# A two-layer transformer block on one core: the program's head with the second pair's low parts behind the ninth score step, later weights cast earlier, shift rows moved by head, and one normalisation shared by two engines

## What is computed

```python
x = L0_attn_x                                   # (4, 1024, 128) float32
x = x + _layernorm(attention(_layernorm(x)))
x = x + _layernorm(lora_experts(_layernorm(x)))

def attention(x):                               # 16 heads of 64
    xn = layer_norm(x) * g + b
    q, k, v = xn @ wq + bq, xn @ wk + bk, xn @ wv + bv
    scores = q k^T / 8;  scores = where(tril(ones, k=-1), -inf, scores)
    return softmax(scores) @ v @ w0 + b0 + x
```

## Time and profile before

| what | us |
|---|---|
| three runs | 996.43, 996.57, 998.40 (median 996.57) |
| the profiled execution | 996.35 |
| its span on the core | 994.6 |
| PE, PEld busy | 955.1, 600.4 |
| DVE, ACT, POOL busy | 634.6, 536.1, 701.7 |

### The profile page before, as it was taken

How to read it: one execution, slowest core, us unless ns; L and a number is a source line. 1 busy time by engine, 2 the same in 40 slices (tenths; PEclk the granted TensorE clock), 3 DMA queues, 4 the chain that set the end, 5 groups by cost and what they waited for, 6 DMA issues and landing times.

```text
span 994.6 us, 20388 instructions
## 1 busy us (share of the span) xinstructions
PE 955.1 (96%) x7662; PEld 600.4 (60%) x7662; DVE 634.6 (64%) x1869; ACT 536.1 (54%) x729; POOL 701.7 (71%) x517
## 2 busy tenths in 40 slices
PE   8899999999999999999999999999999999999995
PEld 3555656666666565666665666666666666666563
DVE  6666555555667657566757666756666665756377
ACT  5355546555455565765454565665455546555443
POOL 6378766667767767786676877776588676776752
PEclk9999999999999999999999999999999999999998
DMA  4001110011111000002100201110110200000110
GB/s 114 23 1 24 22 23 14 12 23 44 24 23 44 19 6 23 23 23 45 23 5 20 66 23 23 23 23 2 44 23 24 66 23 23 3 23 24 23 44 21
DMA packets 61837, 26.94 MB, mean 27 GB/s; under 512 B 39084, under 2 KB 53804, under 8 KB 61740
## 3 DMA queue, kind: packets, MB, share of 16 engines
q1 hardware_dynamic: 61708, 25.64, 11.0%
q10 hardware_dynamic: 32, 0.00, 0.0%
HBM read 22.76 MB, written 2.35 MB: 25 GB/s over the span
## 4 chain that ended last, share of the span: by engine, by line
PE 71%; POOL 14%; DVE 7%; ACT 4%; issue 3%; DMA 0%; POOLq 0%; ACTq 0%; DVEq 0%
PE po L770 20%; PE st L755 14%; POOL total L520 12%; PE st L680 9%; PE sc L718 7%; PE st L836 5%; PE st L750 5%; PE sc L780 3%; ACT ring L1048 3%; PE st L695 2%; DVE sc L1246 2%; PE st L696 1%; PE st L697 1%; POOL first_moments L477 1%; DVE least L1249 1%
## 5 line engine op out<-in xcount | busy, mean ns | idle before, releaser
L520 POOL TENSOR_TENSOR total<-total,ring 128x1024 f32<-128x1024 f32 (+1 forms) x313 | 539.0, 1722 | 246.2 <-PE po L770 204.7
L1246 DVE CUSTOM_DVE_ANT_0 sc<-sc,key_mask 128x512 f32<-128x512 f32 (+1 forms) x496 | 230.4, 522 | 142.2 <-PE sc L718 139.4
L1048 ACT ACTIVATE ring<-st 128x1024 f32<-128x1024 f32 (+1 forms) x256 | 228.5, 918 | 167.4 <-PE st L755 149.0
L1249 DVE TENSOR_REDUCE least<-sc 128x1 f32<-128x512 f32 x268 | 170.4, 678 | 74.9 <-PE sc L718 73.1
L770 PE MATMUL po<-ring,v_sb 128*64 128x512 f32 (+3 forms) x1280 | 210.7, 467 | 0.0
L755 PE MATMUL st<-q_high,k_low 64*128 64x512 f32 (+3 forms) x768 | 177.1, 447 | 0.0
L770 PEld LDWEIGHTS po<-ring,v_sb 128*64 128x64 f32 x1280 | 86.9, 137 | 129.5 <-issue 124.4
L718 PE MATMUL sc<-k_high,q_high 64*128 64x512 f32 (+3 forms) x768 | 135.5, 383 | 10.3 <-DVE least L1246 5.2
L755 PE MATMUL st<-q_high,k_high 64*128 64x512 f32 (+3 forms) x768 | 136.9, 343 | 0.0
L755 PE MATMUL st<-q_low,k_high 64*128 64x512 f32 (+3 forms) x768 | 136.8, 341 | 0.0
L718 PEld LDWEIGHTS sc<-k_high,q_high 64*128 64x128 f32 x768 | 69.0, 185 | 81.5 <-issue 64.4
(11 more groups left out here) (184 smaller groups left out, 1256.9 us busy)
## 6 DMA issues: line engine op xcount, KB each, us to landing
inv_row<-sums_dram SPq DMA_DIRECT2D x62, 256.0 KB, 3.9
x_a<-x SPq DMA_DIRECT2D x4, 512.0 KB, 5.1
sums<-sums_row SPq DMA_DIRECT2D x124, 2.0 KB, 2.1
x_b<-x SPq DMA_DIRECT2D x3, 512.0 KB, 5.7
out<-res_b SPq DMA_DIRECT2D x3, 512.0 KB, 4.7
total<-w_pairs SPq DMA_DIRECT2D x1, 1152.0 KB, 6.8
shift_row<-shift_t SPq DMA_DIRECT2D x62, 4.0 KB
x_a<-x SPq DMA_DIRECT2D x2, 256.0 KB, 3.0
```

What stands on the lines that cost most here:

```text
L520: nc.gpsimd.tensor_tensor(so_far, so_far, tile_of(n, s)[:, :, col:col + w], ALU.add).then_inc(s_add, 1)
L1048: nc.scalar.activation(tile_of(n, s)[:, :, 0:w], st[s % 2][:, :, 0:w], ACT.Exp, scale=SCALE).then_inc(s_exp, 1)
L1246: last = nc.vector.tensor_tensor_reduce(bank[:, col:col + w], bank[:, col:col + w], key_mask[:, 0:w], -1.0, 3e38, ALU.add, ALU.min, least[ ...
L1249: last = nc.vector.tensor_reduce(least[:, h, a:a + 1], bank[:, col:col + w], AX.X, ALU.max, negate=True)
```

## The change

It touches five places of the head; the loop over slots is the same.

1. **Order of DVE behind step 8.** `high_w(slice(2, 8), 1)` leaves this place. The low parts of k and q of pair 1 come ahead of `maxima(1, 0)`, k first.
2. **Later weights.** The casts of `high_w(slice(2, 8), 1)` now stand between the two `x_low` instructions, and POOL's `low_w(1, ...)` ahead of `first_shifts`.
3. **Norm shared.** Of the four tiles that DVE normalised, ACT takes two (`s_z_part`). PE's four unread matmuls between the transposes go, and six stand behind them in place of four.
4. **Rows.** `shift` is laid out so that a half's high and low parts of one head stand on eight neighbouring partitions once transposed; one transfer moves both rows (32 instead of 64 counts).
5. **PE.** Pair 1's projections stand in threes between the score steps, without unread matmuls between them. Two unread stand ahead of `("m", 0, 0)`, and four in place of eight ahead of slot 0.

```diff
@@ -208,6 +208,8 @@
         shift = sb("shift", [P, 2, 2, QB], bf16)
+        shift_halves = shift[:].rearrange("p h s i -> p (h s i)").rearrange("p (h a s i) -> p h a s i", h=2, a=2, s=2)
         shift_t = sb("shift_t", [32, P], bf16)
@@ -269,7 +271,7 @@
         s_half, s_later_keys = sem("s_half"), sem("s_later_keys")
-        s_shift_half, s_first_row = sem("s_shift_half"), sem("s_first_row")
+        s_shift_half, s_first_row, s_z_part = sem("s_shift_half"), sem("s_first_row"), sem("s_z_part")
         s_score, s_max, s_shift, s_shift_row = (sem(n) for n in ("s_score", "s_max", "s_shift", "s_shift_row"))
@@ -333,10 +335,9 @@
         def move_first(eng, half, h):
-            for k in range(2):
-                row, i = h * D + k, h * 16 + k * 8 + 4 * half
-                eng.dma_start(shift_row[0][row:row + 1, half * HALF:(half + 1) * HALF], shift_t[i:i + 4, :]
-                              ).then_inc(s_first_row, 16)
+            i = h * 16 + 8 * half
+            eng.dma_start(shift_row[0][h * D:h * D + 2, half * HALF:(half + 1) * HALF], shift_t[i:i + 8, :]
+                          ).then_inc(s_first_row, 16)
@@ -488,15 +489,15 @@
-                blocks = slice(4 * half, 4 * half + 4)
                 if half:
                     pool.wait_ge(s_max, 2 * BLOCK_STEPS)
                     wait_filled(pool, "m", 0, 0)
                 else:
                     pool.wait_ge(s_least, 1)
                 part = least[:, :, QB + 4 * half:QB + 4 * half + 4]
-                pool_link(nc.gpsimd.tensor_copy(shift[:, :, 0, blocks], part))
-                last = nc.gpsimd.tensor_tensor(shift[:, :, 1, blocks], part, shift[:, :, 0, blocks], ALU.subtract)
+                high, low = (shift_halves[:, :, half, a, :] for a in range(2))
+                pool_link(nc.gpsimd.tensor_copy(high, part))
+                last = nc.gpsimd.tensor_tensor(low, part, high, ALU.subtract)
                 last.then_inc(s_shift if half else s_shift_half, 1)
@@ -593,9 +594,9 @@
             gate_constants()
+            low_w(1, slice(2, 8))
             for half in range(2):
                 first_shifts(half)
-            low_w(1, slice(2, 8))
             pool.wait_ge(s_w_low, 2)
@@ -730,7 +731,7 @@
                     need(s_const, 5)
-                    need(s_first_row, 64 * (1 + half))
+                    need(s_first_row, 32 * (1 + half))
                 elif s == 0:
@@ -897,10 +898,10 @@
             turn_four(z_head, 0, st[0][:, 0, :]).then_inc(s_zt, 1)
-            unread(4)
             need(s_z, 1)
+            need(s_z_part, 1)
             turn_four(z_head, 1, st[0][:, 1, :]).then_inc(s_xt, 1)
-            unread(4)
+            unread(6)
@@ -915,25 +916,21 @@
             score(0, 3)
-            project(1, 1, range(0, 2))
+            project(1, 1, range(0, 3))
+            score(0, 4)
+            project(1, 1, range(3, 6)).then_inc(s_fill[0], 1)
+            score(0, 5)
+            project(0, 1, range(0, 3))
+            score(0, 6)
+            project(0, 1, range(3, 6)).then_inc(s_fill[1], 1)
+            score(0, 7)
             unread(2)
-            score(0, 4)
-            project(1, 1, range(2, 4))
-            unread(2)
-            score(0, 5)
-            project(1, 1, range(4, 6)).then_inc(s_fill[0], 1)
-            unread(2)
-            score(0, 6)
-            project(0, 1, range(0, 3))
-            unread(2)
-            score(0, 7)
-            project(0, 1, range(3, 6)).then_inc(s_fill[1], 1)
             fill(("m", 0, 0), "sc")
             score(0, 8)
             unread(6)
             score(1, 0)
             fill(("m", 0, 1), "sc")
-            unread(8)
+            unread(4)
             for t in SLOTS:
@@ -1091,7 +1088,7 @@
                     if part or n == 1:
-                        act.wait_ge(s_first_row, 64 * (1 + n))
+                        act.wait_ge(s_first_row, 32 * (1 + n))
                     reach(act, s_shift_row, 32 * (n - 1))
@@ -1109,6 +1106,9 @@
             norm_apply(1, z_head, x_a, low).then_inc(s_z0, 1)
+            act.wait_ge(s_root, 2)
+            act.wait_ge(s_x[1], 16)
+            norm_apply(1, z_head, x_a, high[:2]).then_inc(s_z_part, 1)
             act.wait_ge(s_cols, 16 * 2)
@@ -1335,11 +1335,13 @@
             dve.wait_ge(s_root, 2)
-            for t in high:
+            for t in high[2:]:
                 root, moved = root_and_moved(1, t)
                 last = nc.vector.tensor_scalar(z_head[:, t, :], x_a[:, t, :], root, moved, ALU.mult, ALU.add)
             last.then_inc(s_z, 1)
             for a in range(2):
+                if a == 1:
+                    high_w(slice(2, 8), 1)
                 half = slice(a * 512, (a + 1) * 512)
@@ -1421,12 +1423,11 @@
                     least_of_two(0)
-            high_w(slice(2, 8), 1)
+            dve.wait_ge(s_high, 4)
+            take(("k", 1, 0), 0)
+            take(("q", 1, 0), 1)
             maxima(1, 0)
-            dve.wait_ge(s_high, 4)
-            take(("q", 1, 0), 1)
-            take(("k", 1, 0), 0)
             for t in SLOTS:
                 c, i = divmod(t, PAIRS)
                 for g in range(3):
```

## The result

The kernel after takes 994.47 us in the median of 17 runs (993.83 to 995.12); the kernel before, beside it, 996.57 (996.37 to 998.40). The ratio is 0.9974, with a 95% interval from 0.9967 to 0.9981: faster by 2.1 us, where 3.0 were forecast. The times of the kernel before lie in two groups, twelve from 996.37 to 997.18 and five from 997.96 to 998.40, so its median depends on how many fall into each. The profiled execution took 994.58 us, its span is 992.8, 1.8 under the one before.

What follows compares the result with a forecast made beforehand. The head's chain up to c0 was taken as the bound, DVE alone from 32.30 to 37.23 us. Terms 0.27 + 0.61 + 1.34 + 0.82 = 3.04 us gave a median of 993.5, range 992.8 to 995.0.

Steps and rivals of the forecast that it cites:

- (a): Rival, head: casts and POOL's masks hold each other up; gain 2.5 to 2.6 us, 994.1; chance 0.18 together with (d).
- (b): Rival, between the two x_low: later weights land late, x_low 1.1 us late; gain 1.7, 994.9; chance 0.13.
- the first term: Between the two x_low: with norm shared and casts in the wait, second x_low at 12.55 for 12.82, 0.27 us gained.
- PE's order: Score steps 5 to 8: PE reaches steps 6 and 7 earlier, so DVE waits less; 0.61 us gained.
- the casts: Behind score step 8: the casts of the later weights leave DVE's chain, where they lay whole; 1.34 us gained.
- the swap: Behind step 8: k and q ahead of S(1,0)'s maxima, cutting DVE's wait for S(1,1) from 1.50 to 0.68; 0.82 us gained.
- The norm: Start of the head: sharing tiles starts the second transpose 0.5 us earlier; ACT's two more tiles cost nothing.
- POOL's order: POOL ahead of the first shift: subtractions end about 27.6, shift asked for at 27.9; costs nothing, 0.3 us to spare.
- The rows in one transfer: Ahead of T(0,0): one transfer there at 32.3, T(0,0) doesn't wait for it; nothing gained or lost.
- T(0,0) neither by the transfer nor by POOL: Sign behind step 8: T(0,0) at 33.0; release by the transfer or by POOL would show the prediction wrong.
- (c): Rival, PE: fewer unread matmuls and new idle stretches drop the clock to 1.2 GHz; slower, up to 1000.3; chance 0.04.
- (d): Rival, behind step 8: S(1,1) sets the pace, the swap's 0.82 falls away; gain 2.2, 994.3; chance 0.18 with (a).

Runs made afterwards that it cites:

- e2: Kernel after with the two casts of the later weights moved behind q_low and k_low of pair 0 on DVE: 994.71 us, ratio 0.9974.
- e1: Kernel after with 18 unread matmuls at the start in place of 23: 993.79 us, ratio 0.9967.
- e3: Also e3_both: kernel after with 18 unread matmuls at the start and the two casts moved behind q_low and k_low of pair 0: 993.65 us, ratio 0.9964.
- e11: e3 with DVE's order behind step 8 changed to k_low, maxima of S(1,0), q_low: 993.35 us, ratio 0.9961.
- e4: Kernel after with 28 unread matmuls at the start in place of 23: 995.98 us, ratio 0.9990.
- e6: Kernel after with the swap undone, maxima of S(1,0) again ahead of q_low and k_low of pair 1: 997.07 us, ratio 1.0002.

## Why the prediction was right, and where its size was off

**Direction and range.** Faster by more than 0.2% had 0.81, and 994.47 lies between 992.8 and 995.0. The likeliest value was 993.5, 0.97 too low, and the band given to the forecast itself, 993.0 to 994.0 with 0.63, was missed. The time fell between those of rivals (a), 994.1, and (b), 994.9, and neither was its cause: the range was wide enough for reasons that didn't come, which is in part luck.

**The step that was mis-sized** is the first term, "0.27 gained" from the norm and the casts. It took the first transpose's start, 8.46, and so the first `x_low` at 10.60, as given, since the change doesn't touch what stands ahead of them. They vary from execution to execution: 23 unread matmuls at 0.43 or 0.22 us each stand ahead of the transpose, and in the eight profiles with 23 of them that followed, the kernel after's among them, it began between 9.03 and 9.97. The profile of before had by far the earliest, 8.46, and the earliest start of DVE's norm too, 8.22 (8.35 to 8.88 in the thirteen others). In it the wait between the two `x_low` was 1.53 us long because DVE was ready early and the second transpose, which waited for z, late. With the first transpose at 9.6 the second comes right behind it, the wait is 0.58 (e2), and 1.34 us of casts don't fit. Measured, the term was −0.98 between the two profiles. Of these 1.25 us between forecast and measurement, the late transpose makes 1.14 (first `x_low` at 11.74 for 10.60), the casts' being slower 0.11 (2.06 from `x_low` to `x_low` for 1.95). With 18 unread matmuls (e1) the second `x_low` came as long behind the start of the norm as the sum has it: its arithmetic was right, and what it took as given wasn't. Had the kernel before met the same late start, it would have lost about 0.2 itself (9.64 + 3.37 = 13.01 for 12.82), so against a kernel before that starts as late the gain in the head is 2.0 us.

**Step by step.** Between the profiles of before and after, counted from the second `x_low`: step 8's maxima begin 0.63 earlier (0.61 forecast for PE's order), the three pieces behind them end another 1.34 earlier (1.34 forecast for the casts), and `c0` another 0.81 (0.82 forecast for the swap); together 2.78 for 2.77. Undone one at a time the three make 0.58, 1.40 and 1.31. The last two overlap, since k_low covers a wait of 0.42 for S(1,0) that the casts covered before. The norm: nothing while the casts stand there. POOL's order: nothing in the kernel after, as forecast, where 0.55 of POOL's waiting were left, but 0.2 in e3 and e11, whose heads are earlier. The rows in one transfer: nothing, as forecast. S(1,1) released by DVE's maxima at 36.24, T(0,0) neither by the transfer nor by POOL: as forecast. The gain of the head arrived behind it.

**The rivals.** (a), casts and masks holding each other up, is there in small: from `x_low` to `x_low` the eight profiles with the casts there took 1.94 (e4) to 2.17 (e1) for the 1.95 of the sum, and the kernel after has a select of 1.01, POOL's masks about 1.05 late, hidden by the wait of 0.55. The Trainium skill's rule (SBUF — State Buffer, "Who interferes with whom"), that one blocks the other for the whole instruction, agrees with the select, which began beside the cast and ended just behind it. It cost a small part of the 0.6 allowed for, because few of POOL's instructions met the casts. (b) was nearest in size, a second `x_low` 1.1 late, but its cause, late weights, wasn't there: the casts started right behind the first `x_low`. (c) did not occur in the kernel after. e6 shows that it was nearer than the prediction had it: there the clock fell behind a wait of 2.37 us, where the wait ahead of T(0,0) in the kernel before was 1.48. (d) fell: the swap gave at least what it was said to.

**What stays open.** Behind `c0` the profiles took 951.2 to 952.2 us (e6 953.4). The clock near the end doesn't explain it. The stretches of e3_both, of the kernel after and of the kernel before:

```profile
955.00:960.00 5.00, 5.00 (x42) 0.78 0.00 0
960.00:965.00 5.00, 5.00 (x36) 0.88 0.01 3
```
```profile
955.00:960.00 5.00, 4.92 (x53) 1.00 0.00 0
960.00:965.00 5.00, 5.00 (x42) 1.00 0.01 3
```
```profile
955.00:960.00 5.00, 4.92 (x61) 1.00 0.01 4
960.00:965.00 5.00, 5.00 (x32) 0.66 0.01 3
```

The kernel before had a clock of 0.66 there and took 951.4 behind `c0`, as the kernel after did at 1.00; e3_both took 952.2. The 953.4 of e6 have a second fall of the clock in them, behind a wait that every one of the fourteen profiles has, of 1.73 to 1.85 us, which ends between 532 and 537 us. PE of e6 and its stretches, then PE of the kernel before:

```profile
536.45 0.79 PE L719 MATMUL sc<-k_high,q_high 64*128 64x512 f32 x2 [1.76 <-DVE least L1246]
```
```profile
537.00:538.00 1.00, 1.00 (x8) 0.50 0.00 0
538.00:539.00 1.00, 1.00 (x10) 0.50 0.00 0
```
```profile
535.72 0.50 PE L718 MATMUL sc<-k_high,q_high 64*128 64x512 f32 x2 [1.78 <-DVE least L1246]
```

In the other thirteen the granted clock stayed at 1.00 there. So a wait of that length can cost the clock in one execution and not in another, and its length alone doesn't decide it. The fall in e6's head may be of the same kind: it has not been shown that a wait of 1.5 us is safe and one of 2.4 is not. What else decides it wasn't tried. Nor was it shown why the first matmuls change their rate when they do, or how often the start is early in timed runs: the medians' distances (0.7 for e1, 0.8 for e3, none for e2) agree with the heads only roughly.

## What to carry to other kernels

A wait in one profile is a place for work only if both its ends are fixed by the program; where one end hangs on something that varies between executions (here how fast the first matmuls go), look at that end in several profiles before work is put there, or put the work into a wait whose two ends move together. Of several pieces that must follow one another on one engine, put each just ahead of whom it alone holds up: k_low, maxima, q_low gave 0.7 us over k_low, q_low, maxima in the profiled heads (0.3 between the medians, whose intervals overlap). And matmuls that only keep the engine busy may have two prices: too many ahead of real work delay it (e4, `c0` 1.0 later), and too few leave a longer wait, behind which the clock fell in the one execution profiled (e6).

## What the runs showed of the hardware

The first matmuls of the program ran at 0.43 us for 512 columns and later at 0.22, and the change came at different moments in the same instructions: 18 begun by 7.2 us in one execution, 12 to 16 in the others. The granted clock read 1.00 all the while, so it can't be used for the very start. A wait of 2.37 us with PE idle, in a head otherwise busy, was followed 1.2 us after the restart by about three us at a granted clock of 0.50 to 0.72, 1.1 us longer than the same stretch at 1.00; waits of 1.48 (two profiles) and 1.51 (one) were not followed by one. A wait of some 1.8 us in the middle of the program was followed by such a fall in one execution of fourteen, and there it was 1.76 us long, when others had up to 1.85 and none. With twelve unread matmuls fewer the kernel after kept a granted clock of 1.00 up to 46 us, in both its profiles. A small select on POOL that began 0.10 behind a cast of 0.97 us on DVE ended 0.14 behind it, after 1.01 us in place of 0.29.
